# Splitting the next quad's inputs behind the four masks of a step instead of in front of them

## The reference

```python
q = (x @ Wq + bq).reshape(b, n, H, HD)      # k and v alike
scores = einsum('bqhd,bkhd->bhqk', q, k) / sqrt(HD) + mask
out = einsum('bhqk,bkhd->bqhd', softmax(scores), v).reshape(b, n, d)
x = layernorm(x + out @ Wo + bo)            # layer 0
x = layernorm(x + out)                      # layer 1
```

## Time and profile before

| | |
|---|---|
| median of 3 runs | 3168.12 us (3167.33 to 3170.53) |
| the profiled execution | 3165.01 us, of which the span shown is 3163.2 us |
| PE busy | 2999.1 us, 95% of the span |
| DVE, ACT, POOL busy | 59%, 49%, 43% |
| chain of work that ended last | PE 53%, SP's queue 14%, DVE 12%, DMA 10%, POOL 4% |
| mean granted TensorE clock | 0.97 of full speed |

### The profile page before, as it was taken

The page is one execution under the profiler, slowest core; times in us unless marked ns, Lnnn a source line. Parts: engine busy times, 40 slices in busy tenths (PEclk is TensorE's granted clock), DMA queues, the critical chain, the costliest instruction groups (busy, mean ns, idle before and its releaser), DMA issues.

```text
span 3163.2 us, 58261 instructions
## 1 busy us (share of the span) xinstructions
PE 2999.1 (95%) x18956; PEld 2536.4 (80%) x18956; DVE 1850.6 (59%) x7060; ACT 1557.8 (49%) x5135; POOL 1354.6 (43%) x1285
## 2 busy tenths in 40 slices
PE   7999999999999999999999999999899989999995
PEld 5888888888888888888888877777777777777774
DVE  4556565656565565656566565555556555555655
ACT  4535354544445353545454555455445545554553
POOL 3445555555555454554544333333333333333332
PEclk9999999999999999999999999999999999999997
DMA  5354434444444444344454544554454455455445
GB/s 181 93 142 113 134 107 134 118 123 131 115 137 113 140 115 134 107 134 117 124 149 132 158 119 138 147 138 126 142 155 117 137 147 139 125 144 153 117 137 147
DMA packets 411010, 417.71 MB, mean 132 GB/s; under 512 B 46113, under 2 KB 308513, under 8 KB 410657
## 3 DMA queue, kind: packets, MB, share of 16 engines
q1 hardware_dynamic: 409408, 413.32, 46.5%
q10 hardware_dynamic: 1296, 0.67, 0.1%
HBM read 145.37 MB, written 103.81 MB: 79 GB/s over the span
## 4 chain that ended last, share of the span: by engine, by line
PE 53%; SPq 14%; DVE 12%; DMA 10%; issue 6%; POOL 4%; ACT 1%; DVEq 0%; POOLq 0%; ACTq 0%
PE ring L320 23%; PE ring L328 22%; SPq L235 7%; DVE prob L579 6%; SPq L218 5%; PE ring L363 4%; DMA out<-x 4%; PE ring L352 4%; DMA x_raw<-x_feat 4%; POOL xt_lo L732 3%; DVE turned L597 2%; DMA at_lo<-x_bias 2%; POOL prob L742 1%; DVE x_res L627 1%; SPq L203 1%
## 5 line engine op out<-in xcount | busy, mean ns | idle before, releaser
L479 ACT ACTIVATE prob<-prob,neg_max 128x128 f32<-128x128 f32 x2048 | 791.7, 393 | 259.4 <-DVE neg_max L579 259.4
L742 POOL TENSOR_TENSOR prob<-prob,inv_sum 128x512 f32<-128x512 f32 x512 | 522.2, 1041 | 645.3 <-DVE inv_sum L587 645.3
L459 ACT ACTIVATE k_all<-ring,bk_col 128x512 f32<-128x512 f32 x256 | 311.2, 1216 | 661.7 <-PE ring L320 661.5
L732 POOL TENSOR_TENSOR xt_lo<-x_raw,xt_hi 128x512 fp32r<-128x512 f32 x254 | 331.9, 1316 | 607.6 <-DVE xt_hi L554 607.6
L554 DVE CAST xt_hi<-x_raw 128x512 fp32r<-128x512 f32 x254 | 196.5, 794 | 545.7 <-DMA x_raw<-x_feat 545.7
L579 DVE CUSTOM_DVE_ANT_0 prob<-ring,mask 128x128 f32<-128x128 f32 x2048 | 440.1, 283 | 116.5 <-PE ring L352 116.4
L466 ACT ACTIVATE q_all<-ring,bq_col 128x512 f32<-128x512 f32 x256 | 176.7, 690 | 486.2 <-PE ring L320 486.2
L328 PE MATMUL ring<-w_hi_v,xt_hi 128*128 128x512 f32 x1024 | 406.9, 397 | 8.3 <-DVE neg_max L579 8.3
L597 DVE STREAM_TRANSPOSE turned<-prob 128x512 f32<-128x512 f32 x512 | 347.4, 697 | 114.8 <-POOL prob L742 110.2
L320 PE MATMUL ring<-xt_hi,w_hi_k 128*128 128x512 f32 x1024 | 399.4, 390 | 13.6 <-DVE w_lo_k L542 13.6
L328 PE MATMUL ring<-w_hi_v,xt_lo 128*128 128x512 f32 x1024 | 399.4, 390 | 0.0
(11 more groups left out here) (63 smaller groups left out, 4786.3 us busy)
## 6 DMA issues: line engine op xcount, KB each, us to landing
prob_t<-turned SPq DMA_DIRECT2D x1024, 128.0 KB, 2.8
x_res<-x_tok SPq DMA_DIRECT2D x256, 256.0 KB, 3.6
x_raw<-x_feat SPq DMA_DIRECT2D x254, 256.0 KB, 3.4
x_feat<-x_turned SPq DMA_DIRECT2D x512, 64.0 KB, 2.1
x_tok<-x_bias SPq DMA_DIRECT2D x128, 256.0 KB, 2.3
at_lo<-x_bias SPq DMA_DIRECT2D x512, 64.0 KB, 2.1
out<-x SPq DMA_DIRECT2D x128, 256.0 KB, 3.7
prob<-w_k SPq DMA_DIRECT2D x2, 512.0 KB, 6.7
```

The source lines that it names most:

```text
L459: act.activation(k_all[:, m, :].rearrange("p (b j n) -> p b n j", b=QB, n=SQ), ring[K_BANK[m]][:].rearrange("p (b n j) -> p b n j", b=QB, ...
L479: last = act.activation(prob[b][:, i, n, :], prob[b][:, i, n, :], ACT.Exp, bias=neg_max[b][:, i, n:n + 1], scale=-1.0, accum_out=row_sum[b ...
L732: pool.tensor_tensor(features(xt_lo[s % 2], b), raw_view(raw), features(xt_hi[s % 2], b).bitcast(F32), ALU.subtract).then_inc(x_lo_set, 1)
L742: pool.tensor_tensor(prob[b][:, i], prob[b][:, i], inv_sum[b][:, i, :].unsqueeze(2).to_broadcast([P, NC, NODES]), ALU.mult).then_inc(norm_ ...
```

## The change

The four `x_high` of the next quad keep their place in front of the masks in step 0 alone. In steps 1 to 62 they stand behind the fourth mask and in front of `turn_blocks(s, 0)`. Nothing else is edited, and no instruction is added or removed.

```diff
@@ -689,7 +689,7 @@
                 if s == 0:
                     first_low(6)
                     first_low(7)
-                if s + 1 <= LAST:
+                if s == 0:
                     for b in range(QB):
                         x_high(s + 1, b, x_raw[b % 2])
                 if lp is not None:
@@ -698,6 +698,9 @@
                     mask_scores(s, 2, lp)
                     invert_sums(s, 0)
                     mask_scores(s, 3, lp)
+                    if 0 < s < LAST:
+                        for b in range(QB):
+                            x_high(s + 1, b, x_raw[b % 2])
                     turn_blocks(s, 0)
                 for b in range(QB):
                     if la == 0:
```

## The result

The changed kernel takes 3584.3 us (median of 4 runs, 3581.4 to 3588.8) against 3169.0, a ratio of 1.131 (95% interval 1.129 to 1.133): 415 us slower. The forecast was 3679 with a range of 3600 to 3790, so direction and places were right, and the size was too large by 95 us, 16 us outside the range.

What follows compares the result with a forecast made beforehand. PE was taken to bound layer 0 fully and, with mask waits, layer 1. Losses of 382.9, 9.8, 9.4 and 108.8 sum to 511; on 3165.0 that is 3676, or 3679 as median, range 3600 to 3790.

Steps and rivals of the forecast that it cites:

- What bounds the kernel, and what the wait costs: PE busy throughout layer 0; in layer 1 mask waits cost 3.55 us a step plus 2.15 for the lower clock.
- Masks at 1.3, casts at 8.2, the load of graph 2 at 10.2: Times in us from the start of a step's scores at which DVE's masks, moved casts and SP's load would start.
- That last piece I take whole from layer 1, where it runs in the same way: From SP's issue of graph 2's load to the end of the last x_low: 7.25 us, low end 6.60, high end 7.9.
- half as slow: Rival: graph 2's load there much earlier or POOL's work reordered; layer 0 loses 5 us a step, some 3440; chance 3%.
- The wait in layer 0, 10.2 us: PE stands still ahead of project_out for DVE's at_lo, 10.2 us (9.5 to 10.9) in each step with a projection out.
- The clock, 2.15 us a step: PE runs at 1.2 instead of 2.4 GHz for some us after standing still, costing 2.15 us a step on average.
- Layer 1: ACT's third attention copy holds up the values, 7.3 us: ACT's copy waits for turn_attention, delaying the values of graph 1; PE loses 7.3 us at the second key unit.
- The sum: 382.9 for layer 0, 9.8 for step 32, 9.4 for step 33, 108.8 for layer 1: 511 us more.
- The bias additions come onto the path: On POOL in layer 0, four add_out_bias (4.97 us) behind a late x_low delay normalise_probs, ending at 22.4.
- A second loop through SP in layer 1, just short of binding: turn_blocks through SP's carries to the last normalisation, 31.5 us, 0.5 us of slack; rival that it binds: 3770 us, 12%.
- The Trainium skill's rule to wait late: Issue a DMA early, wait late: masks would cover the landing; the trace disagreed for half of the loads.

Runs made afterwards that it cites:

- the kernel with graphs 2 and 3 last: Kernel before, with graphs 2 and 3 split behind turn_blocks and the first attention operations, their x_low behind normalise_probs(s, 0): 2997.0 us, ratio 0.946.
- the two kernels with company: Changed kernel with one, or three, 256 KB copies inside device memory issued just ahead of the load of graph 2: 3667.0 us and 3830.6 us.
- the run with the bias additions first: Changed kernel with the four bias additions on POOL put in front of x_low: 3456.9 us, ratio 1.092 against the kernel before.
- the run that freed ACT: Changed kernel with the first two turn_attention of layer 1 put in front of the moved casts: 3603.0 us, ratio 1.140 against the kernel before.
- graphs 2 and 3 behind the masks: Changed kernel with graphs 0 and 1 split before the masks, 2 and 3 behind: 3300.3 us; also with bias additions ahead of the last two x_low: 3075.6 us.

## Why the prediction was right in direction and too large

- *What bounds the kernel, and what the wait costs.* Right. The wait of the earlier trace rows is gone after the change, and the kernel with graphs 2 and 3 last shows that it and its clock loss were worth 170 us.
- *Masks at 1.3, casts at 8.2, the load of graph 2 at 10.2.* Right to 0.1 us in the step read.
- *"That last piece I take whole from layer 1, where it runs in the same way": 7.25 us.* This is the step that failed. It does not run in the same way. In layer 1 before, SP had issued stores, loads and transposed blocks in the few us ahead of the load; after the change SP has been waiting and nothing is in flight (a busy share of the DMA engines of 0.99 there, 0.00 here). The piece measured 6.10, below the 6.60 I held for the low end. The landing was shorter by 3.84 - 2.66 = 1.18 us, which is all of the 1.15, and the two kernels with company show that it moves with what is in flight. My range was built from two rows of the kernel before, both with company, so it could not hold this, though the earlier trace rows had loads that landed in 2.5 us. In the sum the step is worth 62 x 1.15 = 71 of the 95 us. The rival "half as slow" had named an earlier graph 2 as its cause; that came, but at 1.15 us a step and not at the 7 it was priced at.
- *The wait in layer 0, 10.2 us.* 8.72. Of the 1.5 too much, 1.15 is that piece; 0.05 the bias additions, 0.08 from `normalise_probs` to `at_lo`, and 0.2 the last product of PE, which I did not take off.
- *The clock, 2.15 us a step.* 1.99 in layer 0 and 2.38 in layer 1: right as a size, but it is no constant (3.03 behind the shorter wait of the run with the bias additions first).
- *Layer 1: ACT's third attention copy holds up the values, 7.3 us.* The place was right, the second key unit. It could start 6.1 us late, again 1.2 less. A step was forecast at 49.74 and took 48.41.
- *The sum.* Layer 0: 31 x (63.52 - 61.88) = 51 us too much; layer 1: 29 x (49.74 - 48.41) = 39; together 90 of the 95.
- *The bias additions come onto the path.* Shown: with them ahead of `x_low` 4.89 us of the wait went.
- *A second loop through SP in layer 1, just short of binding.* Right as far as shown: lengthened by 1.9 us, it bound in the run that freed ACT. In the changed kernel itself the masks of layer 1 kept their 1.3.
- *The Trainium skill's rule to wait late* ("DMA: Bandwidth & Descriptors", Rules for kernel authors) did not carry the case for the whole move, as argued. For graphs 2 and 3 alone, the first of whose loads is issued as the masks start in the last kernel (2253.19, the first mask at 2253.24), it holds: the casts wait for nothing and the time falls to 2997.

## What to carry to other kernels

When a step with its own handshake (cast, second cast, load into the freed buffer) is moved as a block, look at what of it was already in flight at the old place. Here half of it was free to stay in front and start the loads, and the other half could go last. Ask on every engine that follows the moved step what stands behind it in that engine's list; here the bias additions on POOL and the copies on ACT carried the delay to PE, though the code of neither was touched. And a duration of a DMA belongs to the traffic that it ran in: for a place where the queue will have run dry, hold the range open downwards.

## What the runs showed of the hardware that I had not expected

- The landing of one 256 KB load was 2.66 us with nothing ahead of it, 3.08 with one copy of 256 KB ahead, and 4.86 with three (single steps; the ranges are given above).
- The price of a PE wait in granted clock did not grow with the wait in layer 0: waits of 3.83, 8.72, 9.77 and 12.5 us were followed by losses of 3.03, 1.99, 2.34 and 2.3 us a step (steps of 58.03, 61.88, 63.28 and 65.95 us, less 51.17 and the wait). Shortening a wait from 8.7 to 3.8 us gave back 3.85 us, not 4.89. Shorter waits cost less: in layer 1 a mean wait of 3.55 us cost 2.15 (the kernel before) and one of 51.3 / 29 = 1.77 cost 0.94 (graphs 2 and 3 behind the masks), of which some 0.3 is not the clock, since a step there with a wait of 0.98 us at a granted clock of 1.00 took 41.61, 0.34 more than 40.29 and the wait. Two waits in one step, of 4.38 and 3.10 us, cost 4.55 together.
